# ACT centres the tiles behind the attention output, and PE turns them a round later

## What is computed

```python
x = _layernorm(x + _L1_attn_ref(x, w_q, w_k, w_v, w_o), axis=-1)
x = _layernorm(x + _L1_ffn_ref(x, w1, w1_scale, w3, w3_scale, w2, w2_scale), axis=-1)

def _layernorm(x, axis=-1, eps=1e-05):
    m = jnp.mean(x, axis=axis, keepdims=True)
    v = jnp.var(x, axis=axis, keepdims=True)
    return (x - m) / jnp.sqrt(v + eps)

# the end of the attention block
return jnp.einsum('bse,oe->bso', out, w_o)

# the start of the MLP: each block of 128 columns is scaled by its largest value and back
amax = jnp.max(jnp.abs(xb), axis=-1)
scale = amax / FP8_MAX + 1e-12
xq = (xb / scale[:, :, None]).reshape(T, K)
xdq = (xq.reshape(T, K // BS, BS) * xs[:, :, None]).reshape(T, K)
```

## Time and profile before

| What | Before |
|---|---|
| Median of three runs | 1966.54 us (1963.94 to 1967.96) |
| The profiled execution: time, span | 1963.11 us, 1961.4 us |
| Busy: PE, DVE, ACT, POOL | 1712.8, 1564.5, 834.6, 759.3 us |
| The stage `out_and_normalise` | from about 1352 to 1450 us |
| Longest busy groups of the stage on DVE | `out_xq` 17.8 us in 64, `all_X` (centring) 13.0 us in 16 |

### The profile page before, as it was taken

One profiled execution on the slowest core, in us unless ns is written; L12 is line 12 of the kernel. 1 busy time (PEld: TensorE's weight loads), 2 busy tenths in 40 slices (PEclk: granted clock), 3 DMA queues, 4 the chain that ended last, 5 costly groups with the idle time before them and its releaser, 6 DMA issues. The chain is left out here.

```text
span 1961.4 us, 24773 instructions
## 1 busy us (share of the span) xinstructions
PE 1712.8 (87%) x7777; PEld 1046.9 (53%) x7777; DVE 1564.5 (80%) x2845; ACT 834.6 (43%) x1407; POOL 759.3 (39%) x466
## 2 busy tenths in 40 slices
PE   7888878776898995997688888888879999999997
PEld 2232323223677774885233333334658788788786
DVE  7999999999868997731788888884977766776678
ACT  6646464443315774321367777775211111111112
POOL 5897989896167996301130000000031321320200
PEclk8999989999999997998699999999989999999999
DMA  6334252321049995744443333320000000000002
GB/s 151 95 115 130 82 145 79 102 80 59 7 174 381 410 410 203 275 182 177 115 123 92 92 92 92 92 71 4 1 33 32 33 20 14 33 33 1 1 1 86
DMA packets 110706, 211.67 MB, mean 108 GB/s; under 512 B 18907, under 2 KB 35675, under 8 KB 109681
## 3 DMA queue, kind: packets, MB, share of 16 engines
q1 hardware_dynamic: 105457, 193.30, 30.1%
q0 software_dynamic: 5120, 16.78, 2.5%
HBM read 144.95 MB, written 62.65 MB: 106 GB/s over the span
## 5 line engine op out<-in xcount | busy, mean ns | idle before, releaser
L2043 DVE TENSOR_REDUCE att_top<-att_first 128x1 f32<-128x512 f32 x512 | 332.1, 686 | 69.7 <-PE att_first L1923 62.1
L560 DVE TENSOR_TENSOR_SCAN ssm_h<-ssm_da,ssm_dbx 128x512 f32<-128x512 f32 x256 | 304.4, 1205 | 6.6 <-ACT ssm_da L423 6.1
L293 POOL TENSOR_TENSOR ssm_dbx<-ssm_u,ssm_bbc 128x2048 f32<-128x2048 f32 x63 | 285.0, 4524 | 45.9 <-DVE ssm_h L560 45.5
L647 PE MATMUL ssm_y<-ssm_hc,all_ident 128*128 128x512 f32 x396 | 227.2, 662 | 70.9 <-DVE ssm_hc L509 65.3
L2005 ACT ACTIVATE att_prob<-att_second 128x1024 f32<-128x1024 f32 x256 | 248.0, 1022 | 86.6 <-PE att_second L1943 81.3
L423 ACT ACTIVATE ssm_da<-ssm_dt,ssm_minus_a 128x512 f32<-128x512 f32 x256 | 176.7, 690 | 195.1 <-DVE ssm_h L560 194.8
L2297 POOL TENSOR_TENSOR pairs_raw<-pairs_raw,pairs_scales 128x512 f32<-128x512 f32 x42 | 42.2, 1040 | 505.6 <-DMA pairs_raw<-in_w 505.6
L2427 ACT ACTIVATE ffn_silu<-ffn_pg 128x256 f32<-128x256 f32 x112 | 43.2, 386 | 408.0 <-PE ffn_pg L129 408.0
L1923 PE MATMUL att_first<-att_ks,att_qs 48*128 48x512 f32 x512 | 133.5, 511 | 64.8 <-DVE att_top L2043 50.1
L127 PE MATMUL ffn_pg<-pairs_wh,last_XH 128*128 128x512 f32 x448 | 177.1, 395 | 1.7 <-PEq L2101 1.7
L128 PE MATMUL ffn_pg<-pairs_wl,last_XH 128*128 128x512 f32 x448 | 177.0, 395 | 0.0
(11 more groups left out here) (340 smaller groups left out, 3759.2 us busy)
## 6 DMA issues: line engine op xcount, KB each, us to landing
all_X<-in_w SPq DMA_DIRECT2D x33, 769.0 KB, 7.2
ssm_bbc<-brow_dram SPq DMA_DIRECT2D x64, 256.0 KB, 4.2
ssm_cbs<-crow_dram SPq DMA_DIRECT2D x58, 256.0 KB, 3.5
mlps_raw<-in_w SPq DMA_DIRECT2D x16, 769.0 KB, 7.4
att_qs<-qk_dram SPq DMA_DIRECT2D x192, 64.0 KB, 2.2
att_ks<-qk_dram SPq DMA_DIRECT2D x192, 64.0 KB, 2.2
sorted_x<-ssm_zero SPq DMA_DIRECT2D x47, 256.0 KB, 3.7
sorted_y<-exp_y SPq DMA_DIRECT2D x47, 256.0 KB, 7.4
```

What stands on the lines that cost most here:

```text
L293: nc.gpsimd.tensor_tensor(dbx[:, n % 2], u[:, n // STATE % 2], bbc[:, n % RING, :].unsqueeze(1).to_broadcast([P, KC, NB]), ALU.mult).then_ ...
L560: nc.vector.tensor_tensor_scan(h[:, n % 2, c, :], da[:, i % 2, :], dbx[:, n % 2, c, :], 0.0, ALU.mult, ALU.add).then_inc(h_ready, 1)
L647: pe.matmul(y[:, c, :], g.ident[:], hc[:, k % 2, :], start=(m == 0), stop=(m == STATE - 1)).then_inc(y_own, 1)
L2043: nc.vector.tensor_reduce(top[w % 2][:, qt, item:item + 1], p_first[first_place(m) % FIRSTS][:], AX.X, ALU.max).then_inc(max_done, 1)
```

## The change

On ACT a new function `centre` makes `all_X` from `out_po` as rstd * x + shift, where the shift, minus mean times rstd, is a new instruction on DVE (`shift`, one element per partition) in place of DVE's `centre`. `centre` comes first in ACT's rounds. PE's `turn_x` and ACT's `x_hi` go from one round back to two, DVE's `x_lo` from two to three, and DVE's list is reordered: the low parts now stand right behind the shift, and `largest` to `quantised` follow one another. No arithmetic is left out.

```diff
+        moved = sb("moved", [P, TILES])
...
-        xh_ready, xl_ready = sem("xh_ready"), sem("xl_ready")
+        xh_ready, xl_ready, shift_ready = sem("xh_ready"), sem("xl_ready"), sem("shift_ready")
...
@@ PE
-                each(n, (-1, turn), (0, outputs), (1, turn_x))
+                each(n, (-1, turn), (0, outputs), (2, turn_x))
...
@@ ACT
+            def centre(t):
+                act.wait_ge(shift_ready, t + 1)
+                nc.scalar.activation(g.X[:, t, :], po[t % RING][:], ACT.Identity, bias=moved[:, t:t + 1],
+                                     scale=rstd[:, t:t + 1]).then_inc(x_ready, 1)
+
...
-                each(n, (-1, turned_hi), (0, root), (1, x_hi))
+                each(n, (1, centre), (-1, turned_hi), (0, root), (2, x_hi))
...
@@ DVE
-            def centre(t):
+            def shift(t):
                 dve.wait_ge(std_ready, t + 1)
                 nc.vector.reciprocal(rstd[:, t:t + 1], std[:, t:t + 1]).then_inc(rstd_ready, 1)
                 dve.wait_ge(rstd_ready, t + 1)
-                nc.vector.tensor_scalar(g.X[:, t, :], po[t % RING][:], mv[:, t, 0:1], rstd[:, t:t + 1], ALU.subtract,
-                                        ALU.mult).then_inc(x_ready, 1)
+                nc.vector.scalar_tensor_tensor(out=moved[:, t:t + 1], in0=mv[:, t, 0:1], scalar=-1.0, in1=rstd[:, t:t + 1],
+                                               op0=ALU.mult, op1=ALU.mult).then_inc(shift_ready, 1)
...
-                each(n, (1, centre), (1, largest), (-1, turned_lo), (1, block_scale), (1, quantised), (2, x_lo), (0, variance))
+                each(n, (1, shift), (-1, turned_lo), (3, x_lo), (1, largest), (1, block_scale), (1, quantised), (0, variance))
```

## The result

The changed kernel takes 1973.65 us (median of eight runs, 1969.86 to 1976.48); the kernel before takes 1963.7 us in the eight runs beside it. The ratio is 1.0047, with a 95% interval from 1.0038 to 1.0056: 9.2 us slower, 7.5 to 11.0 (the two medians by themselves are 9.95 apart). On another occasion on one chip with three of the experiments the ratio was 1.0059 (1.0046 to 1.0073). The prediction was 9.6 us slower.

What follows compares the result with a forecast made beforehand. DVE was taken as the bound. Twelve full rounds (+9.0), two early rounds (+0.75, +0.15), the last (-0.46) and the end (+0.14) summed to +9.6 us: median 1976.1 us, 0.5% slower, range 1969 to 1983.

Steps and rivals of the forecast that it cites:

- Later turn of x on PE: PE turning the quantised tile a round later: removes PE's 0.83 us wait per round, worth 0 by itself.
- Duration of the centring on ACT: Centring activation on ACT: 0.74 us, from a 0.597 us copy plus 0.071 for each of two operands; bounds 0.58 and 0.81.
- Low part starts after the aggregate: DVE's low part of the turned tile starts 2.04 us after the aggregate's end, once ACT's high part is done.
- DVE's wait in it: DVE idle before the low part of the turned tile, released by ACT's high part: 1.3 us in 14 rounds.
- Full round: One full DVE round, 2.04 plus 4.26 us: 6.30 us against 5.55 before, 0.75 more.
- The bound: In the changed stage DVE limits: it is waited for and hardly waits; its round takes 5.55 us, PE could do 4.7.
- The queue: On ACT centring stands ahead of the turned tile's high part, so DVE stands through two activations: 0.75 us more per round.
- the third rival: Clock falls inside the stage as PE waits longer; five slow rounds add 15 us, giving 1991; chance 0.06.
- its lead of 5 us: PE's outputs are ready 5 us before their use in the following round, which absorbs one short clock fall.
- its price of 3 us for each low round: At half clock PE's 4.7 us become 9.4 at most and set the round: 3 us more each, once PE's lead is gone.
- Behind the stage: Next stage's matmuls after PE's idle: same cold start, taken as 0, with 2 us each way.
- The level: Starting time for the forecast: median of the three runs shown, 1966.54 us, giving 1976.1 us.

Runs made afterwards that it cites:

- The lags alone: Kernel before with PE and ACT handling x two rounds back, DVE's low part of x three, DVE still centring: ratio 0.9997, -0.6 us.
- the old lags in the best order: The fastest kernel with turn_x and x_hi one round back and x_lo two, as in the kernel before: ratio 1.0020, +3.9 us.
- the one that centres on DVE: Kernel before with the change's lags, x_lo ahead of the reciprocal on DVE, x_hi ahead of the root on ACT: ratio 0.9973, -5.3 us.
- the fastest kernel: Changed kernel with both high parts before ACT's root, turned_hi one round earlier, and x_lo first on DVE: ratio 0.9954, again 0.9952.
- the kernel with the early high part: Changed kernel with both high parts before ACT's root and the turned tile's made one round earlier: ratio 0.9963, -7.3 us.

## Why the prediction was right

| Step | Predicted | Measured |
|---|---|---|
| Later turn of x on PE | 0 | 0.1 us alone (fifteen rounds 0.6 less, the end of the stage 0.7 more) |
| Duration of the centring on ACT | 0.74 (0.58 to 0.81) | 0.78 |
| Low part starts after the aggregate | 2.04 | 2.05 |
| DVE's wait in it | 1.3 in 14 rounds | 1.33 in 14 |
| Full round | 6.30 | 6.33 |
| From the first statistics to the next stage | +9.6 | +9.9 |
| Time against the kernel before | +9.6 | +9.2 (7.5 to 11.0) |

*The bound.* DVE was named by who waits for whom, not by its busy share. The lags alone bear it out: PE's 0.83 us of waiting moved and the rounds stayed at 5.55. One sentence of that step is too strong: the product is not DVE's only input from PE, since both low parts are made from tiles that PE turned. For this change it made no difference, because neither came late; with the old lags in the best order one does, and DVE waits 0.56 us a round behind PE's turn of x and ACT's high part of it.

*The queue.* That DVE would stand through two activations came from the two written orders, and its length from start-to-start times of the earlier trace rows. The exchange of two entries on ACT took it back, and the doubled centring lengthened it by its own step.

*The centring's duration* was 0.04 us too low. By the row with one per-partition operand each costs 0.071, and two make 0.74. The Trainium skill's page "ScalarE: Activation LUTs" (section "What ACT_TABLE_LOAD costs") states 93 ns for each, by which the estimate is 0.80; 0.78 lies between the two. ACT's high part of the turned tile thus began 0.03 us later than computed; the crossing to DVE took 0.02 in place of 0.04, and the low part was out by only 0.01.

*The place and not the duration.* The advice of the same page of the Trainium skill to use VectorE for adds and multiplies (section "Rules for kernel authors") would have given the right sign for another reason. The runs do not bear it out for this stage: with the queues in order, the kernel that centres on ACT is 2.6 us (traces) to 4 us (ratios) faster than the one that centres on DVE. That this comes from DVE being the busier engine (57.55 of 60 us from 1365 to 1425 where it centres, 54.27 where it does not) is my reading; the two kernels differ in other places too.

*The clock.* PE's wait rose to 1.56 us a round and the granted clock stayed at 2.4 GHz (1.00 from 1352 to 1450 us), so the third rival did not come true. With the centring done twice PE waited 2.24 us and the clock did fall, at no cost to the rounds. The prediction allowed for that with its lead of 5 us, which absorbs one short fall; its price of 3 us for each low round was an upper bound, and the falls seen there made PE's work 1.6 us longer in place of 4.7. The Trainium skill's page "TensorE: Matmul & The Clock Gate" (section "A second HAM failure mode: psum-queue depth-cycling") tells of a kernel in which short idles between groups of matmuls made the clock swing; the changed kernel's trace does not show this, that of the kernel that centres twice does. The 1.12 us turn at the end of the stage came again, at 1.11:

```profile
1457.23 1.11 PE L2159 MATMUL out_px<-all_ident,out_xq 128*128 128x128 f32 x4 [3.98 <-DVE out_xq L2234]
```

Behind the stage, where I had taken 0, the next stage's first matmul and its fifteenth are 5.61 us apart against 5.03, as the full clock came back three matmuls later. That is 0.6 of the 1.2 us by which the rest is longer; the two profiles of the fastest kernel have 5.09 and 4.63, so it varies by nearly as much without a change.

*The level.* The median I forecast, 1976.1, was reckoned from the median of the three runs shown. The eight runs of the kernel before have 1963.7, so the level was 2.8 us too high and the difference was right within 0.4.

## What to carry to other kernels

Before moving work to an idle engine, write down what stands behind it in that engine's queue and who waits for that: an engine idle for 4 of 6 us still put 10 us into the kernel, because it was idle at another moment. The mend is to place what others wait for into the idle time (here before the root, which waits anyway), and to put a step that needs nothing new in front of each wait. Then repeat the check for every reordering: two of my own expectations missed on exactly this, a high part behind a root and a lag that was free in one order and worth 11 to 13 us in another.

## What the runs showed of the hardware

Instructions of DVE that do not wait for a short one before them start sooner than a dependent one does. With the high part early, the low part came 0.07 us after the start of a 0.16 us shift, where the dependent pair, reciprocal and shift, is 0.20 apart. With the low part of x ahead of the reciprocal, the same shows behind the aggregate (timeline of DVE, second run of the fastest kernel):

```profile
1397.25 0.18 DVE L2207 BATCH_NORM_AGGREGATE out_mv<-out_stats 128x2 f32<-128x6 f32 x1
1397.35 0.66 DVE L2242 TENSOR_TENSOR last_XL<-out_px,last_XH 128x512 fp32r<-128x512 f32 x1
1397.92 0.15 DVE L2211 RECIPROCAL out_rstd<-out_std 128x1 f32<-128x1 f32 x1
```

The low part of x starts 0.08 us before the aggregate ends. In the kernel with the early high part I had computed rounds of 5.03 us, with the low part 0.20 behind the shift; it came 0.07 behind it, and 4.91 was measured. In the fastest kernel I had expected the search for the largest value 1.85 us after the aggregate; it came after 1.69, and the round was 4.76 in place of 4.91.

The clock at the start of the stage has two outcomes, whatever the kernel. In seven of the thirteen profiles the mean granted clock over the stage's first 8 us is 0.79 and the first statistics come after 7.76 to 7.94 us; in the other six it is 1.00 and they come after 6.27 to 6.29 us. What decides between them is not shown.
